# TensorE's order in an attention step: products with Wh first, transposes of the maximum next, new scores last

## The reference

```python
def _gat_layer(x, W, adj):
    proj = x @ W
    Wh, Ws = jnp.split(proj, 2, axis=-1)
    scores = Wh @ Ws.T
    a = jax.nn.softmax(scores, axis=-1) * adj
    out = a @ Wh
    out = out + x
    return jax.nn.leaky_relu(out, NEG_SLOPE)
for l in range(W_stack.shape[0]):      # two layers
    x = _gat_layer(x, W_stack[l], adj)
```

## Time and profile before

| what | value |
| --- | --- |
| median of 3 runs | 1641.16 us (1640.25 to 1642.18) |
| time of the profiled execution | 1643.23 us |
| its span in the trace | 1641.4 us |
| PE busy | 1568.4 us, 96% of the span |
| weight loads (PEld) busy | 1542.8 us, 94% |
| DVE, ACT, POOL busy | 1183.7 (72%), 1086.6 (66%), 996.9 us (61%) |
| attention layers in the trace | from about 550 us to the end |

### The profile page before, as it was taken

How to read it: one execution, slowest core, us unless ns; L and a number is a source line. 1 busy time by engine, 2 the same in 40 slices (tenths; PEclk the granted TensorE clock), 3 DMA queues, 4 the chain that set the end, 5 groups by cost and what they waited for, 6 DMA issues and landing times.

```text
span 1641.4 us, 34734 instructions
## 1 busy us (share of the span) xinstructions
PE 1568.4 (96%) x12902; PEld 1542.8 (94%) x12902; DVE 1183.7 (72%) x2138; ACT 1086.6 (66%) x2115; POOL 996.9 (61%) x874
## 2 busy tenths in 40 slices
PE   5899999999999999999999999999999999999984
PEld 5899999999999999999999999999999999999984
DVE  6556767666675677777777778757777777777774
ACT  4679898988984566666666666646666666666653
POOL 1112222222220588888888888838888888888886
PEclk9999999999999999999999999999999999999999
DMA  4124444554430133333333335512333333333332
GB/s 144 39 50 118 118 123 116 126 138 116 119 95 26 53 97 97 98 97 97 97 95 96 96 97 180 166 40 84 98 101 99 97 101 100 97 98 97 98 103 71
DMA packets 88665, 163.35 MB, mean 100 GB/s; under 512 B 9265, under 2 KB 19376, under 8 KB 88240
## 3 DMA queue, kind: packets, MB, share of 16 engines
q1 hardware_dynamic: 60624, 113.41, 23.1%
q0 software_dynamic: 24336, 44.31, 11.0%
q10 hardware_dynamic: 3536, 3.41, 0.6%
HBM read 147.99 MB, written 13.11 MB: 98 GB/s over the span
## 4 chain that ended last, share of the span: by engine, by line
PE 74%; POOL 11%; issue 8%; DVE 4%; ACT 3%; DMA 0%; POOLq 0%; DVEq 0%; SPq 0%; ACTq 0%
PE PS L1116 25%; PE PS L1314 7%; PE PS L1317 7%; PE PS L1316 7%; POOL FR L427 5%; PE PS L1189 5%; PE PS L1186 5%; PE PS L1188 5%; PE PS L1187 5%; PE PS L1185 5%; POOL X L420 5%; DVE AF L941 1%; ACT FR L600 1%; ACT ROW L620 1%; POOL PAB L420 0%
## 5 line engine op out<-in xcount | busy, mean ns | idle before, releaser
L427 POOL TENSOR_TENSOR FR<-AF,FR 128x512 fp32r<-128x512 f32 x338 | 449.8, 1331 | 162.7 <-ACT FR L600 162.7
L1116 PE MATMUL PS<-FR,RB 128*128 128x256 f32 x4056 | 539.9, 282 | 4.1 <-ACT X L582 1.8
L1116 PEld LDWEIGHTS PS<-FR,RB 128*128 128x128 f32 x4056 | 500.6, 188 | 12.6 <-ACT X L582 10.9
L420 POOL TENSOR_TENSOR X<-X,ROW 128x512 f32<-128x512 f32 x294 | 397.1, 1351 | 63.1 <-ACT ROW L610 63.1
L1314 PE MATMUL PS<-FR,RA 128*128 128x256 f32 x1352 | 388.9, 288 | 26.2 <-POOL FR L427 26.1
L1317 PE MATMUL PS<-FR,RA 128*128 128x256 f32 x1352 | 379.6, 281 | 0.0
L1316 PE MATMUL PS<-FR,RA 128*128 128x256 f32 x1352 | 378.9, 280 | 0.0
L1314 PEld LDWEIGHTS PS<-FR,RA 128*128 128x128 f32 x1352 | 254.4, 188 | 37.9 <-POOL FR L427 35.5
L941 DVE TENSOR_TENSOR AF<-PS,AJ 128x512 f32<-128x512 f32 x338 | 231.2, 684 | 79.7 <-ACT PS L594 78.4
L393 POOL DMA_DIRECT2D STGT<-adjt x169 | 90.3, 535 | 296.0 <-PE PS L1189 296.0
L582 ACT ACTIVATE X<-PS 128x512 f32<-128x512 f32 x271 | 161.2, 595 | 159.0 <-DVE AF L916 154.4
(11 more groups left out here) (138 smaller groups left out, 2376.8 us busy)
## 6 DMA issues: line engine op xcount, KB each, us to landing
AJ<-adjt SPq DMA_DIRECT2D x338, 256.0 KB, 2.7
STGT<-adjt POOLq DMA_DIRECT2D x169, 256.0 KB, 3.0
xt_scratch<-ROW SPq DMA_DIRECT2D x12, 512.0 KB, 2.7
RB<-xt_scratch SPq DMA_DIRECT2D x12, 512.0 KB, 4.7
x_scratch<-X ACTq DMA_DIRECT2D x13, 256.0 KB, 2.2
ROW<-x_scratch SPq DMA_DIRECT2D x13, 256.0 KB, 3.1
out<-ROW SPq DMA_DIRECT2D x12, 256.0 KB, 3.3
X<-xt SPq DMA_DIRECT2D x1, 1536.0 KB, 11.4
```

What stands on the lines that cost most here:

```text
L420: nc.gpsimd.tensor_tensor(slot, slot, MB.unsqueeze(1).broadcast_to([P, 2, 256]), ALU.subtract)\
L427: nc.gpsimd.tensor_tensor(LO[g % 2], WA[g % 2], HI[g % 3].bitcast(F32), ALU.subtract)\
L1116: last = nc.tensor.matmul(out, stationary(a, k), moving(b, k), start=(k == 0 and i == 0), stop=(k == K - 1 and i == 2))
```

## The change

In each step of the attention loop PE issues the same instructions with the same semaphore waits in another order. Before: `scores`, `turn_max`, `turn_sum`, `turn_out`, `weigh`. After: `turn_sum`, `weigh`, `turn_max`, `turn_out`, `scores`. `project_q` and `transpose_x` stay first; `turn_max_back`, the Wh projections and `turn_sum_back` stay last. The other engines' programs are the same.

```diff
@@ -1379,17 +1379,17 @@
                     project_q(Q_AT[v])
                 if v == X12_AT:
                     transpose_x(PAIRS - 1)
-                if s is not None:
-                    scores(s)
+                if A_END.get(v) is not None:
+                    turn_sum(A_END[v])
+                if a is not None:
+                    weigh(a)
                 if S_END.get(v - 1) is not None:
                     turn_max(S_END[v - 1])
-                if A_END.get(v) is not None:
-                    turn_sum(A_END[v])
                 b = A_END.get(v - 3)
                 if b is not None and b >= PAIRS:
                     turn_out(b)
-                if a is not None:
-                    weigh(a)
+                if s is not None:
+                    scores(s)
                 if S_END.get(v - 1) is not None and not WH_AT.get(v):
                     turn_max_back(S_END[v - 1])
```

## The result

The changed kernel takes 1791.83 us (median, 1789.91 to 1792.7) against 1640.86 for the kernel before: a ratio of 1.0912, interval 1.0899 to 1.0926. The forecast was 1785 us, 1750 to 1815. Its trace spans 1790.8 us, 149.4 more than that of the kernel before.

What follows compares the result with a forecast made beforehand. PE, 96% busy, was taken as the bound. Ordinary-step waits, block boundaries and edge steps summed to 144.4 us, giving 1787.6 on the profiled execution; less its 2.07 over the median, 1785 us for 1641.16, range 1750 to 1815.

Steps and rivals of the forecast that it cites:

- The loop in ordinary steps: Scores' end to low part to weighing two steps on: 6.54 us per two steps, 3.27 a step against 2.84.
- The boundaries: Once a block, longer links followed weighing by weighing: layer two 46.35 us for 40.35, layer one 47.0 for 41.26.
- Rival 1: Boundary links and `project_q` vanish in PE's idle time: block 42.5 us, total 1682 us; chance 0.04.
- rival 2: Longer boundary links add in full to the ordinary steps' cost: 8.9 us a block, total 1855 us; chance 0.07.
- Rival 3: No slower or faster: without mask behind maximum the chain is 2.77 us; 1615 us, at the least 1641; chance 0.05.
- fold_max: DVE operation at block boundaries, taken at its 1210 ns median; at 424 ns throughout, 19 us would come off.
- The last scores' end: End of layer two's last block, priced like its other full blocks at 6.0 us more each.
- The seam: Between layers: layer two's first block 3.3 us more, plus 1.4; step 186's uncovered `turn_max` wait about 0.9.
- the tail: Last 16 steps, with one part alone: order kept, so they take as long as before.
- rival 4: The granted clock falls to 0.91 with a wait in each step: 49 us more, 1834 us; chance 0.04.

Runs made afterwards that it cites:

- a3: Changed kernel with mask ahead of the maximum on DVE and rounding ahead of the eviction on ACT; 1786.71 us (1.0887).
- a5: Changed kernel with each step's scores made one step early, at the end of the step before, except one item at the layers' seam; 1725.45 us (1.0513).
- a4: Changed kernel with the denominator's addition (`total`) placed between maximum and mask on DVE, lengthening the chain by one operation; 1871.3 us (1.1399).
- a8: Changed kernel with POOL's low part over half its columns, 256 of 512, the other half left out; 1711.15 us (1.0425).
- a1: Changed kernel with the mask ahead of the maximum (and of `fold_max` and `weighted`) on DVE in each step; 1834.08 us (1.118).
- a6: Changed kernel with scores first only in the steps without a weighing (0 to 15 and 185 to 188); 1788.02 us (1.0892).
- a2: Changed kernel with the rounding ahead of the eviction on ACT in each step; 1797.88 us (1.0954).
- a7: Changed kernel with `turn_max` and `turn_out` behind the scores of their step instead of ahead; 1809.1 us (1.1015).
- b3: Kernel before with `turn_max` ahead of the scores of its step; 1669.04 us (1.0169).
- b2: Kernel before with mask ahead of the maximum on DVE and rounding ahead of the eviction on ACT; 1730.48 us (1.0542).

## Why the prediction was right, step by step

The span grew by 149.4 us, the sum had 144.4. I time the blocks from one `project_q` to another, in the timeline. After, `project_q` of steps 22, 178, 195 and 325:

```profile
575.07 1.57 PE L1116 MATMUL PS<-RB,WX 128*128 128x256 f32 x12
...
1136.33 1.59 PE L1116 MATMUL PS<-RB,WX 128*128 128x256 f32 x12
...
1209.51 1.58 PE L1116 MATMUL PS<-RB,WX 128*128 128x256 f32 x12
...
1671.79 1.57 PE L1116 MATMUL PS<-RB,WX 128*128 128x256 f32 x12
```

and the same four before:

```profile
570.80 1.59 PE L1116 MATMUL PS<-RB,WX 128*128 128x256 f32 x12
...
1066.84 1.58 PE L1116 MATMUL PS<-RB,WX 128*128 128x256 f32 x12
...
1130.91 1.59 PE L1116 MATMUL PS<-RB,WX 128*128 128x256 f32 x12
...
1533.74 1.60 PE L1116 MATMUL PS<-RB,WX 128*128 128x256 f32 x12
```

| stretch | the sum, us more | measured |
| --- | --- | --- |
| up to step 22 | 4.9 | 4.3 |
| 12 blocks of layer one, to step 178 | 68.4 | 65.2 |
| the seam, to step 195 | 4.4 | 9.1 |
| 10 blocks of layer two, to step 325 | 60.0 | 59.4 |
| to the last scores' end | 6.7 | 9.0 |
| the tail with weighings alone | 0 | 2.4 |

The mechanism was right. The total's error of 5.0 us is smaller than its parts deserve: three stretches were short by 9.4 us together, three were over by 4.4, and these partly cancel.

- *The loop in ordinary steps* was right, in its links and to 1% in its length: 3.25 us a step. `a3` and `a5` open it in two ways, and `a4` and `a8` move it by what the chain moves.
- *The boundaries* were right where I followed them: 46.2 us a block in layer two (462.28 / 10) for 46.35. In layer one it is 46.8 (561.26 / 12) for 47.0. The sentence that the boundaries "cost about as much as `project_q` gives back" hides how the cost is split. Not all 13 steps of a block pay 0.43 us: `a5`, which restores the ordinary distance, takes 2.9 us a block off and not 5.6, and leaves 3.0 at the boundary.
- *Rival 1 and rival 2* fall by the block periods: 42.5 us for the one, about 49 for the other, 46.2 measured.
- *Rival 3* named one link, the mask behind the maximum. `a1` shows that taking it out does nothing in ordinary steps: the eviction beside it is as long. The price of 2.77 us for that chain was wrong; the verdict on the rival was right for another reason than the one given.
- *`fold_max`* was taken at the median of the earlier trace rows. After, all 26 (ns: least, median, most):

```profile
L926 DVE TENSOR_TENSOR ROW<-AF x26: 425/1133/1145, 538.8 to 1732.1; 128x256 f32<-128x256 f32 x26
```

So POOL's greater idle time did not shorten it by more than 0.08 us, since `subtract` starts at the same place in the boundary. The Trainium skill ("GPSIMD Engine Reference", section 1. Specifications) speaks of contention on shared SBUF interfaces; the row agrees that the operation stays long, and lies near the long end of the range that I gave by it.
- *The last scores' end* was short by 2.3 us. I priced the last block as a full one. It has no `project_q`, whose matmuls fill PE's waits in the others, so there the change would cost more; that is my reading, and no run takes it apart.
- *The seam* was short by 4.7 us and *the tail* by 2.4. For the seam I had the wait for `fold_max` at 0.9 us more and nothing of what follows it. The busy rows (PE, PEld, DVE, ACT, POOL, then the granted clock) of the seam, and of the tail:

```profile
1170.00:1175.00 5.00, 2.40 (x21) 2.20 (x20) 2.53 (x5) 1.31 (x4) 0.00 (x0) 1.00 0.00 0
1175.00:1180.00 5.00, 5.00 (x31) 5.00 (x32) 0.42 (x1) 0.85 (x3) 0.00 (x0) 0.66 0.02 3
...
1750.00:1760.00 10.00, 8.11 (x46) 7.90 (x46) 4.46 (x7) 4.09 (x7) 7.97 (x7) 0.71 0.37 105
```

That is rival 4 after all, in a few short stretches instead of everywhere: two at the seam (the other behind 1189, where 5 us have 0.75) and two in the tail, besides one at the very end, which the kernel before has too. `a6` took the seam's wait and the slow matmuls behind `turn_max` away, 2.9 us of the 4.7; the clock's fall behind PE's next long wait, of 3.4 us for the first low part of layer two, stayed in both.

In the tail the prediction had the order unchanged, and there it was wrong: `turn_out` moved behind the weighing of its step, which here waits 1.80 us for its low part. DVE's `result` waits for `turn_out`, and the next `mask` stands behind `result`. After, and then before:

```profile
1751.25 1.06 PE L1357 MATMUL PS<-IDN,AF 128*128 128x128 f32 x4
...
1752.35 0.69 DVE L999 TENSOR_TENSOR ROW<-PS,ROW 128x512 f32<-128x512 f32 x1 [3.51 <-PE PS L1357]
```

```profile
1601.88 0.68 DVE L999 TENSOR_TENSOR ROW<-PS,ROW 128x512 f32<-128x512 f32 x1
```

The mask starts at 1752.95, though its exponential was done at 1750.50, and POOL's next low part waits 2.03 us for what follows it. Both things are in these 2.4 us, the new place of `turn_out` and the clock, at whose lower level the weighing ahead took 2.56 us (1748.69 to 1751.25) instead of some 1.5. The tail takes 59.3 to 59.8 us in `a1`, `a2`, `a5`, `a6` and `a7`, where `turn_out` stands behind the weighing too and the clock falls near it. It takes 57.3 in the kernel before and in `b3`, which have neither. How the 2.4 us divide stays open.

## What to carry to other kernels

When several engines each run a fixed order, swapping two items on the busiest one changes no work; what it changes is how much of that engine's work lies between a producer and its consumer. Work that distance out for each chain (here 5.7 us to 2.7) and hold it against the chain's measured length (3.4), for the ordinary step and for each of the rarer chains apart, and divide a closed loop's length by the number of steps that it spans. An edit that opens one loop puts something else behind the moved operation: list that too, as `a1`, `a3` and `b2` show. Look at the granted clock of each run as well: a longer wait at a boundary can cost again behind it.

## What the runs showed of the hardware

- TensorE's granted clock stood at full speed in ordinary steps with waits of some 0.4 us a step (45.6 us busy of 50), and fell in single places: in the changed kernel to 0.66 in the 5 us after a wait of 2.60 us, and to 0.71 in 10 us of the tail, that is to its lower level, 1.2 GHz, for part of each. Twelve matmuls took 2.58 us there instead of 1.6. In `b2` and `a3` it fell at most boundaries, behind waits of 1.8 us, and cost 1.5 us a block in layer two; the same wait passed without a fall in other blocks, so a wait's length alone does not tell. Nor does the share of idle time: the tail of the kernel before kept the full clock with PE 6.45 us busy of 10, where its waits are 1.54, 0.67 and 0.47 us, and the changed kernel's, with 3.01 busy of 5 and then waits of 1.54 and 1.80 us, did not. The Trainium skill ("TensorE: Matmul & The Clock Gate", part 1) has the clock fall after idle time; the runs agree in that, and the forecast was wrong to take waits of 1 to 2.6 us as harmless on the strength of that rule.
- A weighing that had to wait starts 0.05 us after the low part's end in 183 of the changed kernel's 200 waits (0.15 us in the others), and its first matmul holds the next one back by 0.1 us (0.39 against 0.28 us long), once for each wait.
